# Two neighbouring FFN products issued as 64-row matmuls, one in each row half of the array

## What is computed

```python
xn = _layernorm(x)
s = attention(xn)          # 16 heads of 16, causal, rotary by position, 256 -> 768 -> 256
gate = einsum('bsd,hd->bsh', xn, wg)     # 256 -> 768
up   = einsum('bsd,hd->bsh', xn, wu)     # 256 -> 768
h = silu(gate) * up
g = silu(einsum('bsh,dh->bsd', h, wd))   # 768 -> 256
return x + s * g
```

## Time and profile before

| | |
|---|---|
| median of 3 runs | 1229.83 us (1229.42 to 1235.92) |
| profiled execution, span of its instructions | 1225.2 us |
| TensorE matmul busy | 1124.7 us, 92% |
| VectorE busy | 1039.1 us, 85% |
| ScalarE busy | 891.3 us, 73% |
| GpSimd busy | 771.0 us, 63% |
| granted TensorE clock, mean | 0.993 |

### The profile page before, as it was taken

How to read it: one execution, slowest core, us unless ns; L and a number is a source line. 1 busy time by engine, 2 the same in 40 slices (tenths; PEclk the granted TensorE clock), 3 DMA queues, 4 the chain that set the end, 5 groups by cost and what they waited for, 6 DMA issues and landing times.

```text
span 1225.2 us, 27668 instructions
## 1 busy us (share of the span) xinstructions
PE 1124.7 (92%) x9484; PEld 455.5 (37%) x9484; DVE 1039.1 (85%) x3124; ACT 891.3 (73%) x1708; POOL 771.0 (63%) x943
## 2 busy tenths in 40 slices
PE   3789989999999999999899999999999998999996
PEld 2223423434343443434334342333434343343433
DVE  6789889988989889989899888898898998989832
ACT  4457777777777777777677777777777786878774
POOL 3537445595837948298564966469483894737672
PEclk9989999999999999999999999999999999999999
DMA  6250042403242150611425033431516115240201
GB/s 174 74 147 12 12 123 76 120 28 114 54 146 57 28 150 22 169 29 53 125 71 133 23 99 68 121 83 28 141 32 171 30 32 146 69 93 18 62 2 52
DMA packets 71281, 97.51 MB, mean 80 GB/s; under 512 B 18398, under 2 KB 44388, under 8 KB 71140
## 3 DMA queue, kind: packets, MB, share of 16 engines
q1 hardware_dynamic: 71072, 95.73, 28.2%
q10 hardware_dynamic: 68, 0.01, 0.0%
HBM read 52.76 MB, written 34.47 MB: 71 GB/s over the span
## 4 chain that ended last, share of the span: by engine, by line
PE 50%; POOL 20%; DVE 14%; issue 6%; ACT 6%; DMA 2%; SPq 1%; POOLq 0%; DVEq 0%; ACTq 0%
PE ring L931 25%; PE acc L922 11%; PE st L871 7%; PE ring L898 5%; POOL xn L579 5%; POOL hf L1629 4%; DVE ring L1294 4%; POOL pexp L1599 3%; ACT pexp L1129 3%; DVE mx_a L1298 2%; POOL hT L1638 1%; DVE parts L1356 1%; POOL hT L1633 1%; POOL yn L1648 1%; PE ring L941 1%
## 5 line engine op out<-in xcount | busy, mean ns | idle before, releaser
L1129 ACT ACTIVATE pexp<-st 128x512 f32<-128x512 f32 x1152 | 624.1, 598 | 139.1 <-PE st L871 136.4
L1294 DVE CUSTOM_DVE_ANT_0 ring<-ring,tri 128x512 f32<-128x512 f32 (+3 forms) x1024 | 470.2, 522 | 40.5 <-PE ring L898 39.6
L1599 POOL TENSOR_SCALAR_AFFINE_SELECT pexp<-pexp 128x512 f32<-128x512 f32 x256 | 158.0, 635 | 341.8 <-ACT pexp L1129 250.8
L1298 DVE TENSOR_REDUCE mx_a<-ring 128x1 f32<-128x512 f32 x512 | 326.9, 682 | 28.1 <-PE ring L898 26.2
L922 PE MATMUL acc<-pexp,v_pad 128*17 128x512 f32 (+3 forms) x3072 | 304.3, 491 | 16.7 <-POOL pexp L1599 14.5
L898 PE MATMUL ring<-k_st,q_st 56*128 56x512 f16 (+4 forms) x1536 | 237.6, 326 | 32.9 <-DVE parts L1356 11.4
L871 PE MATMUL st<-q_st,k_st 58*128 58x512 f16 (+3 forms) x1536 | 234.8, 332 | 6.6 <-ACT pexp L1129 3.4
L871 PEld LDWEIGHTS st<-q_st,k_st 58*128 58x128 f16 x1536 | 61.9, 93 | 275.9 <-ACT pexp L1129 175.7
L1629 POOL TENSOR_TENSOR hf<-ga,ups 128x512 f32<-128x512 f32 x96 | 121.8, 1272 | 10.3 <-DVE ga L1365 8.8
L922 PEld LDWEIGHTS acc<-pexp,v_pad 128*17 128x17 f32 x3072 | 61.4, 96 | 154.6 <-issue 119.6
L1638 POOL TENSOR_TENSOR hT<-hf,hT 128x512 f16<-128x512 f32 x96 | 110.8, 1158 | 6.7
(11 more groups left out here) (155 smaller groups left out, 1430.6 us busy)
## 6 DMA issues: line engine op xcount, KB each, us to landing
parts_scratch<-parts SPq DMA_DIRECT2D x32, 512.0 KB, 3.0
q_st<-parts_scratch SPq DMA_DIRECT2D x62, 192.0 KB, 3.9
k_st<-parts_scratch SPq DMA_DIRECT2D x62, 192.0 KB, 4.4
parts_scratch<-parts SPq DMA_DIRECT2D x32, 256.0 KB, 3.6
xo<-in_x SPq DMA_DIRECT2D x32, 256.0 KB, 3.2
out<-xo SPq DMA_DIRECT2D x32, 256.0 KB, 2.3
xn<-in_x SPq DMA_DIRECT2D x7, 1024.0 KB, 8.1
yn<-yT SPq DMA_DIRECT2D x224, 32.0 KB
```

The lines of the kernel that those rows point to most:

```text
L1129: nc.scalar.activation(pexp[:, GH * (n % NSET) + j, :], st[:, (GH * n + j) % NST, :], ACT.Exp, scale=1.0 / (QK_SCALE * np.sqrt(D))).then_i ...
L1294: top_ = nc.vector.tensor_tensor_reduce(out=src, in0=src, in1=tri[:, CH - w:CH], scale=1.0, scalar=NEG, op0=ALU.add, op1=ALU.max, accum_ou ...
L1298: top_ = nc.vector.reduce_max(dst, src, AX.X)
L1599: nc.gpsimd.affine_select(out=t, in_=t, compare_op=ALU.is_ge, fill=0.0, base=0, pattern=[[0, GH], [1, P]], channel_multiplier=-1).then_inc ...
```

## The change

The slot's list of tasks on TensorE goes through a new function. Two neighbouring FFN tasks are a pair ("twins"): both banks are taken first, and then each product's contraction is cut in row halves. In the first turn the first product uses rows 0 to 63 and the second rows 64 to 127 of all four of its operand pairs; in the second turn the sides are changed, so that each product has seen all 128 rows of each. Between the turns TensorE waits on a new semaphore until the last matmul of either product in the first turn has completed. Both products signal at the end of the second turn. Of 8 matmuls of 128 rows there come 16 of 64 rows, in 8 steps of two, with a weight load for each. No other engine's program changes.

```diff
+def second_twins():
...
+            found = [t for t in tasks_at(kind, slot) if names_of(kind, t)]
+            for n in range(1, len(found)):
+                both = found[n - 1:n + 1]
+                if all(t[0] in ("UPG", "UPU") for t in both) and both[0] not in of[kind]:
+                    of[kind].append(both[1])
+    return of
...
+        twin_half = sem("twin_half")
...
+            def twins(kind, i, both):
+                found = []
+                for t in both:
+                    _, c, m = t
+                    if t == ("UPG", 1, 0):
+                        pe.wait_ge(xc_done, 2 * (i + 1))
+                    dst, ready = take(kind, i, t)
+                    w = w_ga if t[0] == "UPG" else w_up
+                    found.append((dst, ready, [(w[:, kt, m * P:(m + 1) * P], xpart[:, kt, 0:CH])
+                                               for kt in range(2) for xpart in ((xh1, xl1) if c else (xh, xl))]))
+                n = TWINS.at(kind, i, both[1])
+                for turn_ in range(2):
+                    if turn_:
+                        pe.wait_ge(twin_half, 2 * n)
+                    for k in range(4):
+                        for a, (dst, ready, pairs) in enumerate(found):
+                            rows = slice(SIDE * (a ^ turn_), SIDE * (a ^ turn_) + SIDE)
+                            left, right = pairs[k]
+                            mm = nc.tensor.matmul(dst, left[rows], right[rows], start=(turn_, k) == (0, 0),
+                                                  stop=(turn_, k) == (1, 3))
+                            if (turn_, k) == (0, 3):
+                                mm.then_inc(twin_half, 1)
+                            if (turn_, k) == (1, 3):
+                                mm.then_inc(ready, 1)
+            def tasks(kind, i, found):
+                for n, t in enumerate(found):
+                    if t in TWINS.seen[kind]:
+                        twins(kind, i, (found[n - 1], t))
+                    elif found[n + 1:n + 2] == [] or found[n + 1] not in TWINS.seen[kind]:
+                        task(kind, i, t)
...
-                            for t in tasks_at(kind, slot):
-                                task(kind, i, t)
+                            tasks(kind, i, [t for t in tasks_at(kind, slot) if names_of(kind, t)])
```

More of the change, by code:

```diff
@@ L294 @@
       for name in ("TX", "QD", "QK", "UPG+DN", "UPG", "UPU", "LNA", "YT", "FT", "FP", "MT")}
+def second_twins():
+    of = {"pro": [], "epi": []}
+    for kind in ("first", "mid", "last"):
+        of[kind] = []
+        for slot in range(SLOTS):
+            found = [t for t in tasks_at(kind, slot) if names_of(kind, t)]
[4 more added lines that the diff above has]
+    return of
+SECOND = second_twins()
+TWINS = Tally(lambda k, t: [t] if t in SECOND[k] else [])
 def body_before(kind, i):
```

## The result

The changed kernel takes 1269.35 us (median of 4 runs, 1266.35 to 1274.31) against 1230.11 us (1229.42 to 1235.92) of the kernel before, measured beside it: 39.2 us more, a ratio of 1.033 with a 95% interval of 1.030 to 1.0359. The forecast was 1259 us in a range of 1240 to 1272. Medians and ratios here leave out one slow execution, of the kernel before with a longer body (1813.09 us, mean granted clock 0.558). The profiled execution took 1271.52 us, its span is 1269.8 us, and the mean granted clock 0.984 instead of 0.993.

The account below looks back on a forecast made before the run. No engine bounds the whole body: GpSimd behind slot 4, a relay around slot 22, TensorE around slot 26. Terms 11.6 + 10.4 + 4.9 + 1.3 + 1.2 = 29.4 us, on median 1229.83, give 1259; range 1240 to 1272.

Parts of the forecast that it names:

- Who bounds what: GpSimd bounds behind slot 4, a relay of engines around slot 22, TensorE around slot 26; no engine bounds the whole body.
- Partly absorbed: Rival: VectorE gets ahead and frees the second bank by the start; slots 4 and 22 lose 0.74 each; 1246 us, chance 0.22.
- Only TensorE's own time counts: Rival: ScalarE's delay is absorbed and 2.5 us remain; chance 0.10 around 1232 us, 0.02 for under 1224.
- The loads hide: In a pair's steps, 0.10 us weight loads run beside matmuls, even of the same row half, so steps take 0.217 us.
- The rival at 1279: Weight loads don't hide: 0.10 us more for six of eight steps in 33 pairs, 19.8 us more; chance 0.05.
- The middle step: Between a pair's turns, TensorE's wait makes one step 0.44 us instead of 0.217, a stall of 0.24.
- The bank wait: Pairs in slots 4 and 22 start 0.76 and 0.75 us later, when VectorE has freed the second bank.
- Both ready at the end: ScalarE starts 0.42 us after a pair's last step; its operations follow 0.49 apart, exponentials in slot 4 +1.49 us.
- Slot 26: Pair where TensorE is the bound: next scores +0.70 us a body, seven times, 4.9 us.
- Slot 14: Pair without bank wait: +0.36 us in first and last body, 0.1 in each mid body behind GpSimd's stretch; sum 1.3.
- The end table: Three last pairs: 0.24 us stall each and 0.5 for ScalarE behind the last; 1.2 us.
- The clock: Granted clock is 1.00 in the two stretches read, around slots 4 and 26, so no cost was put on it.

Follow-up runs that it names:

- the covered wait: Changed kernel with the scores of half 1 issued between the two turns, so that TensorE's wait is filled; 1269.38 us against 1232.08, ratio 1.0319.

## Why the prediction was right, and 10 us short

The time came out in the range, and the mechanism that makes up most of the loss was the forecast one. Luck has a part: the room above 1259 had been left for the stall's bound and for slot 14, and it was filled in the main by other things.

- **Who bounds what** held for slots 4 and 22, which are 22.0 of the 29.4 us. There the chain goes through ScalarE, the loss is ScalarE's delay, and no later stage absorbs it: GpSimd's idle grew from 3.15 to 4.74 us (forecast 4.6). "Partly absorbed" failed, since VectorE does not get ahead: TensorE still waits 0.93 us for it. "Only TensorE's own time counts" failed with the covered wait.
- **The loads hide.** By the Trainium skill, "TensorE: Matmul & The Clock Gate", Part 3, The mechanism, a load overlaps matmuls in flight only where the row groups differ (the same section also lets one run ahead into a background weight buffer). This trace disagrees with the "only": the second step's load into the first half starts at 535.83, beside that half's matmul from 535.82, and the next step comes after the usual 0.22. The rival at 1279 falls.
- **The middle step** is 0.46 to 0.47, not 0.44: the wait is for the later of two matmuls that start 0.02 apart, 536.49 to 536.93 being 0.44, which the forecast counted from the first. 33 x 0.03 = 1 us.
- **The bank wait** was sized at 0.76 and 0.75 us and is 0.84. From the end of VectorE's read-out to the matmul I took 0.06, as for a load with one wait; it is 535.82 - 535.67 = 0.15, and 0.12 to the load. Two waits now stand ahead of that load, one for each bank. That the second is what takes the 0.09 was not tried by itself. In slots 4 and 22 of seven bodies it makes 14 x 0.09 = 1.3 us, most of the 1.6 by which the two terms were short.
- **Both ready at the end** held to a few hundredths: from 537.60 ScalarE starts 0.41 later (0.42 forecast), and the three operations stand 0.49 and 0.48 apart.
- **Slot 26** held in size, 5.0 for 4.9. The sum hides a spread: alone the pair cost 0.80 in each mid body, not 0.70, and together with the others between 0.38 and 0.82.
- **Slot 14** failed: 3.2 us, not 1.3. The form changes went as forecast, 0.22 into and out of the pair:

```profile
574.28 0.38 PE L918 MATMUL ring<-k_st,q_st 56*128 56x256 f16 x4
574.50 0.38 PE L1092 MATMUL ring<-xh,w_ga 64*128 64x512 f16 x1
...
576.28 0.38 PE L1092 MATMUL ring<-xl,w_up 64*128 64x512 f16 x1
576.50 0.38 PE L891 MATMUL st<-q_st,k_st 58*128 58x512 f16 x2
```

  What failed is the guess of what GpSimd's stretch takes up: 0.27 remain in a mid body, not 0.1, and 0.8 in the first and the last, not 0.36. Before, TensorE's products in `ring` stood idle for GpSimd's normalised tiles by some 0.26 us in each of six bodies (releaser, us in all, times), so that this stretch had no more to give; after the change they wait for them no longer:

```profile
POOL xn L579: 1.6, 6
```

  In the body shown the chain now leaves GpSimd for TensorE at 569.8 and runs through this pair. The experiments show which part is left: in a mid body slot 14 costs at most 0.02 us in the three kernels without a wait between turns, 0.28 with one wait, 0.28 with the wait covered, and 0.54 with two (means of six).
- **The end table** failed: 3.0 us, not 1.2. The forecast priced its stalls and one ScalarE delay, and looked for no bank wait:

```profile
1213.72 0.24 PE L1059 MATMUL ring<-ident,mx_p 128*64 128x128 f16 x1
1214.91 0.37 PE L1092 MATMUL ring<-xh,w_ga 64*128 64x512 f16 x1 [0.95 <-DVE ga L1420]
```

  The first pair's banks are freed late, by `ga` behind the late tanh, and the pair behind it waits 0.95 us for one.
- **The clock** failed: "I put no cost on it" looked at the two stretches with pairs and not at slot 25. It cost 4.5 us in the profiled execution, the largest single error. What it cost in the medians is open, as executions differ in it.

The errors that count sum to 0.8 + 0.8 + 0.1 + 1.9 + 1.8 + 4.5 = 9.9 us, and 29.4 + 9.9 = 39.3 for the two profiled executions.

## What to carry to other kernels

Two products that run side by side need both output banks at their start and give both results at their end: before pairing, look at when the second bank comes free, and at who reads the first product while the second is computed. Here those two cost 1.3 of 1.58 us a pair, while TensorE's own stall cost 0.27. A change that shifts a tuned body by a microsecond can also change the clock in a stretch that it does not touch, so price idle stretches of TensorE elsewhere in the body as a risk, upward.

## What was not expected of the hardware

- Behind the same wait of 1.63 us TensorE's clock stayed at its upper level or fell to the lower one: in one of six mid bodies of the kernel before, in all six when each body was 1.51 us longer, in none with the wait cut to 0.55 us; over all traces in 36 of 64, and in none of 20 behind a wait of 0.97 us or less. Each fall cost about 1.5 us.
- A wait of TensorE for its own last matmul costs ScalarE 0.26 to 0.27 us a time, the same for the first and the second (2.97, 3.24, 3.50), and 64-row work in the gap put the second turn off by no more than 0.01 us (0.45 for 0.44).
- From a release by VectorE to TensorE's load 0.12 us passed, and 0.15 to the first matmul, where two waits stand ahead of the load; with one wait it was 0.06 to the load.
